# A decoder block whose cross-attention general path moves to the program's end, with the second projection inside the last batch's period

## The chip, the core and the metric

The kernel runs on one core of one Trainium2 chip. The metric is the device time of one execution in microseconds. The engines are TensorE (PE in the rows; its weight loads are PEld), VectorE (DVE), ScalarE (ACT), GpSimd (POOL) and SyncE (SP), which here issues every DMA. Each engine runs its own list of instructions in order and waits on semaphores for the others.

## What is computed

A decoder layer for 32 batches of 56 tokens of width 128: self-attention, cross-attention to 1500 context rows with 16 heads of width 8, and eight experts of hidden width 512; each part is added to its input and normalised. Cut to what matters here:

```python
x = layernorm(x + self_attention(x))
x = layernorm(x + cross_attention(x, ctx))       # logits clipped to +-10000; all 1/1500 if any weight is NaN
# experts
probs = softmax(x @ Wr); the two largest count
for e in range(8):
    gate = probs where e is among the two, else 0
    vals, idx = top_k(gate, 560)                  # a capacity per expert
    y[idx] += vals * (relu(x[idx] @ W1[e]) @ W2[e])
x = layernorm(x + y)
```

## The kernel before

**Numbers.** Tokens lie in pairs of batches, `TT` = 112 tokens; `QT` = 4 pairs are a quad of `QC` = 448 tokens, and there are `NQ` = 4 quads. The matrix products of the experts are made of high and low parts: each product costs three matmuls of 448 columns.

**The loop over batches.** After self-attention, `periods` runs `period(b, ...)` for b = -2 to 32 on every engine. A period has `NC` = 12 slots c. In period b, PE makes the scores of batch b (L1063), ACT takes their exponential (L563), PE sums the outputs (L1113, L1117) into bank 6, and between them the maxima and the keys and values of the batches ahead are made (L1049, L1088, L1097). The result of batch b-1 is divided by its sums in period b (ACT copies it at L558, PE spreads the sums at L1076, DVE inverts at L775 and scales at L778). In period 31 nothing is left to prepare for later batches; period 32 only divides the last result.

**The flag.** Then DVE derives from all maxima and sums whether the fast path was valid (L785 to L794), PE sums that over the partitions (L1123), DVE writes `flag_int` (L796), and each engine that has something to do in the general path loads it into a register and branches: the general path (up to L1173 on PE) is only run for a flag of one, and is not run for these inputs. It stands between the loop and all that follows. DVE then releases the rest with `S3["attended"]`.

**Second projection and norm.** For each quad n: `project(n)` on PE (L1179, eight passes), ACT copies with the bias (L617), `turned(n)` turns it (L1186), DVE adds the residual and takes mean and variance (`norm`, L673 to L682), POOL takes the power -1/2 (L493), DVE scales (L687), `transposed(n)` (L1193), ACT makes two copies `x2T` and `x_hi` (L621, L622), POOL makes `x_lo` (L496), and `logits(n)` (L1199). POOL then clears `y_sum` and splits the weights of the first experts (`split_weights`, L503 to L507), whose DMAs SP issues behind the flag.

**Experts.** A unit u is one expert and one quad; there are `UNITS` = 32 units of `FC` = 4 steps. Step (u, f) is `up(u, f)` (three matmuls, L1222 to L1224) and `down(u-1, f)` (three, L1232 to L1234). After each `up`, ACT makes the high part (L637) and DVE the low part (`low_part`, L857). PE may be ahead by little:

```python
pe.wait_ge(S4["hidden_low"], u * FC + (f - 3) + PRIME)     # up
pe.wait_ge(S4["hidden_low"], u * FC + (f + 1) + PRIME)     # down, of unit u-1
```

ACT copies the result of each unit to `results` (L643), POOL multiplies it by the gates (L518), DVE adds it to `y_sum` (L956). In units 0 to 15, which are written out, DVE works at the gates between the low parts: softmax and the two largest (L865 to L897), PE transposes them at step `EARLY` = 10 (L1243), and then a search for the threshold of each expert in `ROUNDS` = 32 rounds: DVE counts (L906), PE sums over the partitions (L1246), DVE takes the decision (L916, L917, L914, later L924, L925). `low_parts(r)` gives the low parts, and so the steps of PE, that stand in a round; 46 steps are shared by the 32 rounds. The final gates go to DRAM and come back broadcast (`gate_rows`); only then can POOL gate anything. Units 16 to 31 are a hardware loop of two passes, in which DVE does two additions in each unit. In the end PE turns `y_sum` (L1265), DVE normalises quad by quad, and SP stores (L394).

## Time and profile before

| what | value |
|---|---|
| device time, median of three runs | 1047.92 us (1046.09 to 1053.0) |
| the profiled execution | 1049.38 us, span 1047.6 us |
| PE busy | 964.7 us, 92% of the span |
| DVE busy | 727.3 us, 69% |
| ACT busy | 636.2 us, 61% |
| POOL busy | 354.5 us, 34% |
| chain that ended last | PE 79%, DVE 7%, issue 5%, POOL 4% |

The profile is one execution, its times count from the start of the span. Busy times of matmuls are modelled and overlap, so the distance between two starts tells more of PE's pace than a duration does. "Issue" in the chain is time in which an engine waited for nothing that the profile shows.

### The profile page before, as it was taken

Reading aid. Unit: us, or ns where it says so; the run is one execution under the profiler, and the core shown is the slowest. Engines: PE = TensorE matmul, PEld = TensorE weight load, DVE = VectorE, ACT = ScalarE, POOL = GpSimd, SP = SyncE. Lnnn points to the kernel's source line nnn. Section 1 sums busy time; section 2 is a strip of 40 time slices with the busy share of each in tenths; the row PEclk is TensorE's granted clock in tenths of the full one; section 3 lists DMA queues with packets and bytes.
Section 4 is the critical chain, followed back from the end, with each engine's and each line's share of the span. In section 5 each row is a group of like instructions: output and inputs, shape, how many; then the busy total and the mean of one; then the engine's idle time right before and its main releaser. Section 6 shows DMA issues by size and latency. Waiting matters only on the chain.

```text
span 1047.6 us, 29217 instructions
## 1 busy us (share of the span) xinstructions
PE 964.7 (92%) x10560; PEld 776.5 (74%) x10560; DVE 727.3 (69%) x1428; ACT 636.2 (61%) x1030; POOL 354.5 (34%) x325
## 2 busy tenths in 40 slices
PE   6579999999999999999999999999995678999993
PEld 5445778778778887787787788877874367989993
DVE  2775777777777777777777677777751457777996
ACT  3303777777777777777777777777763123445551
POOL 7315333322333322333223333223300151117842
PEclk9855999999999999999999999999997859999997
DMA  3058655566655666555666556665441010105201
GB/s 97 0 113 177 133 129 112 121 143 144 143 110 110 137 145 140 128 110 118 150 140 143 110 110 139 143 142 128 90 90 43 0 41 8 34 3 199 88 35 35
DMA packets 41572, 109.55 MB, mean 105 GB/s; under 512 B 15218, under 2 KB 23732, under 8 KB 41524
## 3 DMA queue, kind: packets, MB, share of 16 engines
q1 hardware_dynamic: 41524, 108.93, 46.3%
q8 instruction: 28, 0.46, 0.2%
q14 instruction: 20, 0.16, 0.1%
HBM read 31.32 MB, written 0.97 MB: 31 GB/s over the span
## 4 chain that ended last, share of the span: by engine, by line
PE 79%; DVE 7%; issue 5%; POOL 4%; SPq 2%; DMA 2%; ACT 1%; POOLq 0%; DVEq 0%; ACTq 0%
PE psum L1063 17%; PE psum L1049 17%; PE psum L1113 12%; PE psum L1088 8%; PE psum L1097 8%; PE psum L1117 4%; POOL OS_all L518 3%; PE psum L1179 2%; PE psum L1222 2%; PE psum L1223 1%; PE psum L1224 1%; PE psum L1076 1%; DMA arena<-gate_rows 1%; PE psum L1234 1%; PE psum L1233 1%
## 5 line engine op out<-in xcount | busy, mean ns | idle before, releaser
L752 DVE TENSOR_REDUCE arena<-psum 128x1 f32<-128x500 f32 x672 | 445.6, 672 | 198.9 <-PE psum L1049 198.8
L563 ACT ACTIVATE arena<-psum 125x896 f32<-125x896 f32 x384 | 348.0, 916 | 98.9 <-PE psum L1063 90.9
L1049 PE MATMUL psum<-K_hi,Q_bd 128*128 128x500 f32 x672 | 323.1, 492 | 6.1 <-DVE arena L752 3.5
L462 POOL TENSOR_TENSOR arena<-arena,K_hi 128x500 fp32r<-128x500 f32 x96 | 123.8, 1291 | 399.4 <-ACT K_hi L578 397.5
L1063 PEld LDWEIGHTS psum<-Q_st,K_st 97*125 97x125 f32 x1536 | 221.8, 189 | 30.9 <-issue 10.9
L1063 PE MATMUL psum<-Q_st,K_st 97*125 97x224 f32 x1536 | 241.6, 280 | 2.8 <-ACT arena L563 1.3
L1049 PEld LDWEIGHTS psum<-K_hi,Q_bd 128*128 128x128 f32 x672 | 130.9, 196 | 56.8 <-issue 28.4
L1113 PE MATMUL psum<-arena 125*25 125x168 f32 x3072 | 169.4, 310 | 0.2
L637 ACT ACTIVATE K_st<-psum 128x448 fp32r<-128x448 f32 x128 | 69.7, 545 | 87.2 <-PE psum L1224 86.7
L1117 PE MATMUL psum<-arena 125*9 125x56 f32 x3072 | 117.1, 213 | 0.0
L1088 PEld LDWEIGHTS psum<-WvA,arena 97*125 97x125 f32 x768 | 103.5, 195 | 4.2
L1117 PEld LDWEIGHTS psum<-arena 125*9 125x9 f32 x3072 | 94.2, 91 | 15.6
L1088 PE MATMUL psum<-WvA,arena 97*125 97x128 f32 x768 | 103.9, 280 | 0.0
L1097 PE MATMUL psum<-arena,WkA 97*128 97x500 f32 x186 | 96.6, 601 | 0.8 <-ACT arena L576 0.8
L1113 PEld LDWEIGHTS psum<-arena 125*25 125x25 f32 x3072 | 69.1, 103 | 33.7 <-issue 32.2
L857 DVE SCALAR_TENSOR_TENSOR K_st<-psum,K_st 128x448 fp32r<-128x448 f32 x128 | 75.1, 617 | 15.2 <-ACT K_st L637 14.9
L481 POOL TENSOR_TENSOR Q_st<-arena,four_heads 96x896 fp32r<-96x896 f32 x32 | 53.7, 1678 | 78.3 <-PE psum L1063 57.5
L576 ACT COPY arena<-psum 128x500 f32<-128x500 f32 x93 | 53.8, 578 | 41.2 <-PE psum L1049 21.7
L592 ACT COPY arena<-psum 125x384 f32<-125x384 f32 x96 | 46.7, 487 | 39.6 <-PE psum L1088 36.3
L775 DVE RECIPROCAL arena<-psum 128x112 f32<-128x112 f32 x64 | 53.8, 842 | 19.6 <-PE psum L1076 19.6
L578 ACT CAST K_hi<-arena 128x500 fp32r<-128x500 f32 x93 | 56.7, 609 | 3.0
L1222 PE MATMUL psum<-K_hi,K_st 128*128 128x448 f32 x128 | 51.2, 400 | 6.1 <-issue 4.1
(246 smaller groups left out, 1056.5 us busy)
## 6 DMA issues: line engine op xcount, KB each, us to landing
K_st<-K_hi SPq DMA_DIRECT2D x256, 187.5 KB, 4.7
K_st<-arena SPq DMA_DIRECT2D x128, 187.5 KB, 3.4
arena<-in_ctx SPq DMA_DIRECT2D x32, 562.5 KB, 6.8
arena<-gate_rows SPq DMA_DIRECT2D x8, 896.0 KB, 4.3
arena<-in_L_ffn_W SPq DMA_DIRECT2D x16, 256.0 KB, 3.1
Q_st<-max_row SPq DMA_DIRECT2D x224, 0.5 KB, 1.7
arena<-K_st SPq DMA_DIRECT2D x12, 224.0 KB, 4.8
out<-x_all SPq DMA_DIRECT2D x4, 224.0 KB, 2.5
```

Of the source, the lines that this page charges most:

```text
L462: g.tensor_tensor(low.bitcast(F32R), low, K_hi[:, par, n * KB:n * KB + KB].bitcast(F32), ALU.subtract).then_inc(F["keys_low"], 1)
L563: a.activation(P2[c % NP].rearrange("p (n k) -> p n k", n=2), psum[0:CK, 2 + 2 * (c % 2):4 + 2 * (c % 2), 0:HQ // 2], ACT.Exp)\
L637: a.activation(h_hi[k % 2][:, f], bank[f][:, 0:QC], ACT.Relu).then_inc(S4["hidden_high"], 1)
L752: v.reduce_max(mx[:, n // NB, n % NB:n % NB + 1], bank_of(n)[:, 0:KB], AX.X).then_inc(F["piece_max_taken"], 1)
L857: v.scalar_tensor_tensor(h_lo[k % 2][:, f], bank[f][:, 0:QC], 0.0, h_hi[k % 2][:, f].bitcast(F32), ALU.max, ALU.subtract)\
L1049: mm(bank_of(n)[:, 0:KB], Q_bd[:, p].rearrange("p h q -> p (h q)")[:, 128 * (n // NB):128 * (n // NB) + 128], K_hi[:, p, (n % NB) * KB:(n ...
L1063: last = mm(bank[2 + 2 * (c % 2) + g // 2][0:CK, 4 * S * (g % 2):4 * S * (g % 2) + 4 * S], K_st[0:DC + 1, par, g, c * CK:c * CK + CK], Q_s ...
L1088: last = mm(bank[7][0:CK, 128 * k:128 * k + 128], ctxT2[:, (par + ahead) % 2, CK * q:CK * q + CK], WvA[:], start=True, stop=True)
L1097: mm(bank[7][:, 0:KB], WkA[:], ctxT2[:, par, n * KB:n * KB + KB], start=True, stop=True).then_inc(F["keys_made"], 1)
L1113: mm(bank[6][32 * m:32 * m + V3, 0:3 * S], values[:, k, V3 * m:V3 * m + V3], weights_[:, 3 * S * m:3 * S * m + 3 * S], start=(k == 0), sto ...
L1117: last = mm(bank[6][32 * m:32 * m + V1, 3 * S:4 * S], values[:, k, 4 * V3 + V1 * m:4 * V3 + V1 * m + V1], weights_[:, (12 + m) * S:(13 + m ...
L1222: mm(bank[f][:, 0:QC], w1_hi[p[0]][:, w_cols], x_hi[:, cols], start=True, stop=False)
```

## The change

- The flag, the branches and the general path stand behind the experts. The flag is made on DVE in unit 24 and summed on PE in unit 26. The fast path's experts run for every input, and the outputs are stored; then each engine loads the flag and branches over the general path, which now holds its own copy of projection, norm and experts (`passes[1]`). For it the first norm's result is saved to DRAM (`x1_rows`, 896 KB) ahead of the loop, since the second norm now works in place.
- Projection, norm and transposes of quads 0 to 2 and the logits of quads 0 and 1 stand in period 31, with DVE making the copies that ACT made. Batch 31's sums, the logits of quad 2 and all of quad 3 stand among the first eleven steps of the experts. POOL splits the first weights in period 31, and SP loads them as soon as batch 31's queries are spread.
- The gates' transpose stands at step 22; 44 steps are shared by the 32 rounds. A round's decision is one instruction: `expert_rows` has weight 4 and a matmul with `level` subtracts the capacity beforehand in PSUM, so that the total is positive or negative by more than any candidate, and clamping it between two bounds gives the next candidate. The bounds are made behind the count, one instruction in 23 rounds and two in seven.
- Nothing is in a hardware loop behind the batches. 24 results are held instead of 16 (`held`). DVE's additions begin in unit 20 and are spread over twelve units, at most one after each low part. POOL gates units 0 to 29, DVE itself the last two, from PSUM (`gate`). `y_sum` lies where `x2T` lay, so that the residual is in it from the start: POOL's clearing and DVE's four last residual additions are gone, and `statistics` and `scaled` read PSUM. The last norm begins for quad 0 while units 30 and 31 are open.

The core of the diff, in the order SP, POOL, ACT, DVE, PE behind the constants:

```diff
-EARLY, BETWEEN = 10, 46
+LEAD, EARLY, BETWEEN = 11, 22, 44
+KEEP = 24
+GATED = UNITS - 2
+WEIGHT = 4.0
+ADD_FROM = 20
...
+P_AT, T_AT, X_AT, LOGITS_AT = 3, 5, 9, 11
+P_BANK, T_BANK, X_BANK, Y_BANK = (0, 1, 1, 6), (7, 7, 7, 5), (0, 0, 4, 6), (6, 7, 0, 1)
+FLAG_AT = 24
...
+        y_sum = x2T.rearrange("p (q n) -> p q n", q=NQ)
...
+            sp.wait_ge(S1["normed"], NQ + PRIME)
+            sp.dma_start(x1_rows, x1_all[:]).then_inc(x1_saved, 16)
...
+            sp.wait_ge(F["stacked_spread"], B + PRIME)
...
-            for e in range(NE - 2):
...
+                for e in range(NE - 1):
+                    load_weights(e)
...
+            with sp.If(clamped > 0):
+                sp.sem_inc(second, 1)
+                sp.dma_start(x1_all[:], x1_rows).then_inc(x1_back, 16)
...
-            pool.wait_ge(F["flag_ready"], 1 + PRIME)
...
+                for n in range(GATED):
+                    if n in (8, 18):
+                        split_weights(P, NE - 2 if n == 8 else NE - 1)
+                    e = n // NQ
+                    pool.wait_ge(G_[e % 2], (P.past * (NE // 2) + e // 2 + 1) * 16)
+                    pool.wait_ge(S4["result_copied"], n + 1 + P.base4["result_copied"])
+                    g.tensor_tensor(held(n), held(n), gates[e % 2][:, n % NQ], ALU.mult).then_inc(S4["result_gated"], 1)
+                for n in range(NQ):
+                    power(S4, P.base4, n)
+            pool.wait_ge(F["scores_made"], (B - 1) * NC + PRIME)
+            split_weights(passes[0], 0)
+            power(S3, passes[0].base3, 0)
+            power(S3, passes[0].base3, 1)
+            low_inputs(passes[0], 0)
+            low_inputs(passes[0], 1)
+            power(S3, passes[0].base3, 2)
+            low_inputs(passes[0], 2)
+            power(S3, passes[0].base3, 3)
+            low_inputs(passes[0], 3)
+            experts(passes[0])
...
+                        if u * FC + f == LEAD + 2:
+                            act.wait_ge(S4["logits_shifted"], 1 + P.base4["logits_shifted"])
+                            a.activation(pw[:], pr[:], ACT.Exp).then_inc(S4["exp_done"], 1)
...
+                    if isinstance(b, int) and b == B - 1:
+                        P = passes[0]
+                        if c in (1, 2, 6):
+                            projected(P, (1, 2, 6).index(c))
+                        if c == 3:
+                            dve.wait_ge(x1_saved, 16)
+                        if c in (3, 4, 9):
+                            attended(P, (3, 4, 9).index(c))
+                        if c in (5, 8, 10):
+                            n = (5, 8, 10).index(c)
+                            scaled(P.S3, P.base3["rstd_ready"], n, quads3[n], x1_all[:, tiles(n), :])
+                        if c in (7, 8, 11):
+                            normed(P, (7, 8, 11).index(c))
...
+                for n in range(LEAD):
+                    if first and n == T_AT:
+                        attended(P, NQ - 1)
+                    if first and n == X_AT - 1:
+                        scaled(P.S3, P.base3["rstd_ready"], NQ - 1, quads3[NQ - 1], x1_all[:, tiles(NQ - 1), :])
+                    low_part(n // FC, n // FC, n % FC)
...
-                step(v.tensor_scalar(cand[:], thr[:], 2.0 ** -(s - 1), None, ALU.mult))
-                step(v.tensor_scalar(fac[:], tot, float(CAP), bit, ALU.is_ge, ALU.mult))
-                step(v.scalar_tensor_tensor((cand if s < 22 else thr)[:], fac[:], less, cand[:], ALU.subtract, ALU.add))
...
+                    def bounds():
+                        last_of(v.tensor_scalar(low_high[:], offsets[:, s], cand[:], None, ALU.add))
+                    tot = count(ALU.is_ge, cand[:], bounds)
+                    step(v.tensor_scalar((cand if s < 22 else thr)[:], tot, low_high[:, 0:1], low_high[:, 1:2], ALU.max, ALU.min))
...
+                def gate(n):
+                    dve.wait_ge(G_[1], 16 * (NE // 2) * (P.past + 1))
+                    dve.wait_ge(S4["result_made"], n + 1 + P.base4["result_made"])
+                    v.tensor_tensor(held(n), bank[4 + n % 2][:, 0:QC], gates[1][:, n % NQ], ALU.mult).then_inc(S4["result_gated"], 1)
+
+                def due(u):
+                    return (u + 1 - ADD_FROM) * GATED // (UNITS - ADD_FROM) if u >= ADD_FROM - 1 else 0
+                for u in range(UNITS // 2, UNITS):
...
+                    if first and u == FLAG_AT:
...
+                ended(0)
+                gate(GATED)
+                add(GATED)
+                ended(1)
+                scaled(S4, P.base4["rstd_ready"], 0, quads3[0], total(0))
+                gate(GATED + 1)
+                add(GATED + 1)
+                scaled(S4, P.base4["rstd_ready"], 1, quads3[1], total(1))
+                ended(2)
+                ended(3)
+                for n in range(2, NQ):
+                    scaled(S4, P.base4["rstd_ready"], n, quads3[n], total(n))
...
-                for a2 in range(2):
-                    n = u * 2 + (a2 - UNITS)
-                    dve.wait_ge(S4["result_gated"], n + 1 + PRIME)
-                    dve.wait_ge(S4["result_added"], n - (NQ - 1) + PRIME)
-                    q = (2 * k + a2) % NQ
-                    v.tensor_tensor(y_sum[:, q], y_sum[:, q], results[:, 2 * k + a2], ALU.add).then_inc(S4["result_added"], 1)
...
+                    if isinstance(b, int) and b == B - 1:
+                        P = passes[0]
+                        if c in (1, 2, 5):
+                            n = (1, 2, 5).index(c)
+                            pe.wait_ge(F["outputs_scaled"], (n + 1) * (B // NQ) + PRIME)
+                            if n == 0:
+                                pe.wait_ge(F["piece_max_taken"], B * PIECES + PRIME)
+                            elif n == 1:
+                                pe.wait_ge(F["max_row_ready"], B + PRIME)
+                            else:
+                                pe.wait_ge(P.S3["projected_copied"], n + P.base3["projected_copied"])
+                            project(P, n)
+                        if c in (3, 4, 8):
+                            if c == 3:
+                                pe.wait_ge(F["sums_inverted"], 2 * b + PRIME)
+                            turned(P, (3, 4, 8).index(c))
+                        if c in (7, 8):
+                            crossed(P, (7, 8).index(c))
+                        if c == 9:
+                            pe.wait_ge(P.S3["residual_added"], NQ - 1 + P.base3["residual_added"])
+                        if c in (9, 11):
+                            logits(P, (9, 11).index(c))
...
+            crossed(passes[0], 2)
...
+                def added(n):
+                    pe.wait_ge(S4["result_added"], UNITS - NQ + n + 1 + P.base4["result_added"])
+                    for t in range(QT):
+                        last = t_.transpose(bank[Y_BANK[n]][0:TT, D * t:D * t + D], y_sum[:, n, TT * t:TT * t + TT], ident[:])
+                    last.then_inc(S4["outputs_made"], 1)
...
+                        if first and u * FC + f == 1:
+                            sums(B)
+                        if first and u * FC + f == 2:
+                            logits(P, 2)
+                        if first and u * FC + f == P_AT:
+                            pe.wait_ge(F["outputs_scaled"], B + PRIME)
+                            project(P, NQ - 1)
+                        if first and u * FC + f == T_AT:
+                            turned(P, NQ - 1)
+                        if first and u * FC + f == X_AT:
+                            crossed(P, NQ - 1)
+                        if first and u * FC + f == LOGITS_AT:
+                            logits(P, NQ - 1)
...
+                added(0)
+                for f in range(FC):
+                    down(UNITS - 1, UNITS - 1, f, 1)
+                    if f == 1:
+                        added(1)
+                for n in range(2, NQ):
+                    added(n)
+            experts(passes[0], True)
```

In the order of PE's instructions, the place between the second and the sixth slot of period 31. `OS_all` is the cross-attention's result, `WoP` the projection's weights. Before:

```order
L1063 MATMUL psum<-Q_st,K_st 125x224 x4
L1076 MATMUL psum<-arena,sum_rows 128x224
L1063 MATMUL psum<-Q_st,K_st 125x224 x8
L1113 MATMUL psum<-arena 25x168 x4
L1117 MATMUL psum<-arena 9x56 x4
```

With the change:

```order
L1246 MATMUL psum<-Q_st,K_st 125x224 x4
L1204 MATMUL psum<-arena,sum_rows 128x224
L1246 MATMUL psum<-Q_st,K_st 125x224 x4
L1208 MATMUL psum<-OS_all,WoP 128x448 x4
L1246 MATMUL psum<-Q_st,K_st 125x224 x4
L1208 MATMUL psum<-OS_all,WoP 128x448 x4
L1311 MATMUL psum<-arena 25x168 x4
L1315 MATMUL psum<-arena 9x56 x4
L1311 MATMUL psum<-arena 25x168 x4
L1315 MATMUL psum<-arena 9x56 x4
L1246 MATMUL psum<-Q_st,K_st 125x224 x4
L1216 MATMUL psum<-ident,arena 112x128 x4
```

The projections of quads 0 and 1 stand ahead of the first outputs (L1311, L1315), and the transpose of quad 0 (L1216) behind the fourth slot's scores.

PE right behind the loop. Before:

```order
L1113 MATMUL psum<-arena 25x168 x4
L1117 MATMUL psum<-arena 9x56 x4
L1076 MATMUL psum<-arena,sum_rows 128x224
L1123 MATMUL psum<-arena,ones 128x1
L1125 TENSOR_LOAD flag_int
L1125 ISA x2
L1126 COMPARE_AND_BRANCH
```

With the change:

```order
L1315 MATMUL psum<-arena 9x56 x4
L1224 MATMUL psum<-ident,x_all 128x112 x4
L1334 MATMUL psum<-K_hi,K_st 128x448
L1335 MATMUL psum<-Q_bd,K_st 128x448
L1336 MATMUL psum<-K_hi,K_st 128x448
L1204 MATMUL psum<-arena,sum_rows 128x224
L1334 MATMUL psum<-K_hi,K_st 128x448
L1335 MATMUL psum<-Q_bd,K_st 128x448
L1336 MATMUL psum<-K_hi,K_st 128x448
L1230 MATMUL psum<-Wr_sb,arena 112x8 x4
```

The flag's matmul, load and branch are gone from here; the experts' first `up` (L1334 to L1336) stands right behind quad 2's transpose, and the last sums (L1204) behind it.

DVE at the end of the 23 rounds of the search. Before:

```order
L924 TENSOR_SCALAR arena<-psum,bits 128x1
L925 SCALAR_TENSOR_TENSOR arena<-arena,bits 128x1
L906 TENSOR_SCALAR arena<-arena 128x112
L857 SCALAR_TENSOR_TENSOR K_st<-psum,K_st 128x448
L924 TENSOR_SCALAR arena<-psum,bits 128x1
```

With the change:

```order
L963 TENSOR_SCALAR arena<-psum,low_high 128x1
L934 TENSOR_SCALAR arena<-arena 128x112
L961 TENSOR_SCALAR low_high<-offsets,arena 128x2
L873 SCALAR_TENSOR_TENSOR K_st<-psum,K_st 128x448
L963 TENSOR_SCALAR thr<-psum,low_high 128x1
```

Between a total and the next count (L906, now L934) stands one instruction instead of two, and the bounds (L961) stand behind the count.

## Rows read from the trace of the kernel before

**Rows 1.** Stretches: busy (count) of PE, PEld, DVE, ACT, POOL; clock, DMA, GB/s.

```profile
780.00:797.40 17.40, 14.43 (x291) 11.46 (x290) 1.97 (x4) 11.88 (x16) 0.00 (x0) 1.00 0.01 2
...
808.60:853.00 44.40, 27.39 (x97) 18.03 (x97) 18.95 (x67) 6.71 (x13) 14.73 (x14) 0.69 0.04 12
853.00:860.00 7.00, 7.00 (x21) 6.30 (x22) 4.90 (x10) 2.72 (x5) 4.42 (x4) 0.56 0.47 136
...
869.00:873.00 4.00, 4.00 (x16) 3.63 (x15) 1.82 (x9) 1.21 (x3) 0.00 (x0) 0.57 0.00 0
873.00:941.00 68.00, 64.45 (x338) 58.06 (x338) 51.98 (x181) 31.51 (x58) 13.64 (x12) 1.00 0.06 17
941.00:1026.00 85.00, 84.46 (x418) 78.36 (x419) 73.42 (x103) 45.38 (x86) 54.54 (x42) 1.00 0.28 100
```

**Rows 2.** Chain that ended last, loop's end to experts: start us, us, what.

```profile
797.38 0.35 ACT arena L558
...
803.85 0.55 DVEq L798
...
804.83 3.22 issue
...
818.36 3.01 PE psum L1179 x8
...
852.98 0.71 PE psum L1222
```

**Rows 3.** Timeline, projection and norm: start us, us, engine, line, operation.

```profile
821.20 0.60 PE L1186 MATMUL psum<-ident,arena 128*112 128x128 f32 x4
...
821.84 0.69 DVE L673 TENSOR_TENSOR arena<-psum,x_all 112x512 f32<-112x512 f32 x1 [1.23 <-PE psum L1186]
...
842.18 1.53 PE L1199 MATMUL psum<-Wr_sb,arena 128*112 128x8 f32 x8
```

**Rows 4.** Timeline, PE, two steps apart by one, late in the experts.

```profile
1002.32 0.37 PE L1222 MATMUL psum<-K_hi,K_st 128*128 128x448 f32 x1
...
1003.53 0.37 PE L1222 MATMUL psum<-K_hi,K_st 128*128 128x448 f32 x1
```

**Rows 5.** Groups by line, 941 to 1029 us: busy us, mean ns, idle before.

```profile
L857 DVE SCALAR_TENSOR_TENSOR K_st<-psum,K_st 128x448 fp32r<-128x448 f32 x74 | 42.8, 615 | 10.8 <-ACT K_st L637 10.6
...
L956 DVE TENSOR_TENSOR Qt_all<-Qt_all,OS_all 128x448 f32<-128x448 f32 x31 | 34.8, 1158 | 2.6 <-POOL OS_all L518 2.6
```

**Rows 6.** Timeline, additions with POOL busy beside them, and alone.

```profile
961.45 5.27 POOL L518 TENSOR_TENSOR OS_all<-OS_all,arena 128x448 f32<-128x448 f32 x4
...
964.21 2.99 DVE L956 TENSOR_TENSOR Qt_all<-Qt_all,OS_all 128x448 f32<-128x448 f32 x2
...
1028.84 0.63 DVE L956 TENSOR_TENSOR Qt_all<-Qt_all,OS_all 128x448 f32<-128x448 f32 x1 [1.46 <-POOL OS_all L518]
```

**Rows 7.** Timeline, one round of the search: decision, count, and PE's wait ahead.

```profile
868.32 0.32 PE L1243 MATMUL psum<-ident,arena 112*128 112x112 f32 x1 [2.49 <-DVE arena L897]
...
928.59 0.22 DVE L924 TENSOR_SCALAR arena<-psum,bits 128x1 f32<-128x1 f32 x1 [0.93 <-PE psum L1246]
...
929.10 0.33 DVE L906 TENSOR_SCALAR_CACHE_REDUCE arena<-arena 128x112 f32<-128x112 f32 x1
```

**Rows 8.** Timeline, final gates stored, and POOL's first gating behind them.

```profile
940.98 0.33 SPq L385 DMA_DIRECT2D gate_rows<-arena  x1
...
946.80 9.32 POOL L518 TENSOR_TENSOR OS_all<-OS_all,arena 128x448 f32<-128x448 f32 x8 [10.77 <-DMA arena<-gate_rows]
```

**Rows 9.** Timeline, SP's first DMA behind the branch, and the end.

```profile
804.87 0.37 SPq L375 DMA_DIRECT2D arena<-in_L_ffn_W  x1
...
1026.59 0.37 PE L1232 MATMUL psum<-K_st 128*128 128x448 f32 x1
...
1031.64 0.68 DVE L673 TENSOR_TENSOR arena<-psum,x_all 112x512 f32<-112x512 f32 x1
...
1042.17 2.36 DVE L687 TENSOR_SCALAR x_all<-arena 112x128 f32<-112x128 f32 x8
```

741 lines of the change are left out of this document (399 added, 342 removed).

## The prediction

> **What bounds the kernel now.** I read the stretches first. In the experts' second half PE is busy 84.46 of 85.00 us [rows 1]; its matmuls stand 1.213 us apart from step to step, 1002.32 to 1003.53 [rows 4], which is six matmuls at 0.202. 85.00 / 1.213 is 70 steps, and about that many are there: that stretch runs at PE's pace. The loop is close to PE's pace too, but its last period is not full: 14.43 of 17.40 us. The hole lies between: from 797.40 to 808.60 PE works 1.24 us, from 808.60 to 853.00 only 27.39 of 44.40, at a granted clock of 0.69 (between the levels of 1.2 and 2.4 GHz) [rows 1]. The chain of waits says why: batch 31's copy at 797.38, then DVE's small instructions for the flag until 803.85, then a branch with 3.22 us of "issue", then projections and norms in turn, then the first expert matmul at 852.98 [rows 2].
>
> **The gap goes.** From 797.38 to 852.98 are 55.6 us [rows 2]. All of it leaves its place; what comes back is counted next.
>
> **Period 31 gets longer.** PE now has in it three projections, 3 x 3.0 (the one with eight passes, 3.01 [rows 2]); three transposes into PSUM, 3 x 0.5 (0.60 at a middling clock [rows 3]); two transposes back, 2 x 0.5 by the same row; and the logits of two quads, 2 x 1.0 (1.53 at the low clock [rows 3]; I take two thirds). That is 13.5. PE's idle time there is 17.40 - 14.43 = 3.0 [rows 1], but in pieces that belong to waits on ACT, and two new waits for DVE come (the second transpose needs the bank that DVE reads, the transposes back wait for POOL's power and DVE's scaling), about 2 us in all. I count +14 and let the idle time absorb no more than these waits; bounds 10.5 (all 3.0 filled, no wait) and 18. DVE has little else to do there, 1.97 us of 17.40, and ACT 11.88 [rows 1], so the norm's chain, some 4 us a quad (0.69 for the addition alone [rows 3]), can lie beside scores. The loop ends at 797.4 + 14 = 811.4.
>
> **Behind the loop.** Between the first eleven steps stand quad 2's transpose back 0.5, batch 31's sums 0.5, logits 1.0, quad 3's projection 3.0, transposes 0.5 and 0.5, logits with the level's matmul 1.2, by the same rows: 7.2. Step 3 waits for DVE's inversion and scaling of batch 31, step 9 for the norm of quad 3; DVE has nine low parts of 0.615 [rows 5] in the same time. I add 1.3 for both: +8.5.
>
> **The experts.** Ideal are 4 x 0.6 for unit 0, 124 x 1.213 and 4 x 0.6 for the last `down`, 155.3 us. Before, they took 852.98 to 1026.59 + 2.4 = 1029.0, or 176.0: 20.7 more [rows 2, 9]. Of that I can name: the low clock behind the gap, 21 matmuls in 7.00 us instead of 4.2 [rows 1], 2.8; the wait of 2.49 for the gates ahead of the transpose [rows 7] and 4.00 us for 16 matmuls behind it at a clock of 0.57 [rows 1], 0.8 too many; the counts' own matmuls, 33 x 0.14 = 4.6, where 0.14 is my reading of such a small pair; the rest, some 10, is in the rounds and at the loop's ends. What I take after:
> - the low clock is gone, as PE has no gap ahead of the experts; counts 4.6 stay (the subtracting matmul is one more small one a round, inside this figure's error).
> - At step 22 DVE has had twelve more low parts' time for the gates' work, but begins it later (logits of quad 3 at step 11). The 2.49 becomes about 1.6, and I leave the clock behind it at full.
> - The rounds: a decision after a total is now one instruction of 0.22 and not two; between the decision at 928.59 and the count at 929.10 lay 0.51 [rows 7], so some 0.25 a round leaves DVE's serial chain and 0.2 comes back for `bounds`, off the total's path. PE waits for a total's round only where low parts run out; I give the rounds 2.5 in all (0 to 6).
> - The additions. Before, 31 in 85 us took 1.158 each on average [rows 5]; alone one takes 0.63, and two beside POOL's four gatings of 5.27 took 2.99, 1.5 each [rows 6]. Now all 30 lie in twelve units, 2.5 a unit. A unit of DVE is 4 x 0.58 (0.615 with its share of the contention [rows 5]) + 2.5 x 1.17 = 5.25, against PE's 4 x 1.213 = 4.85. POOL begins to gate at about 917 (below) and has 30 x 1.32 [rows 6] + two splits of 5 = 50 us, so it is busy until some 966, which covers units 20 to 27: 8 x 0.4 = 3.2. The flag's chain in unit 24 is ten small DVE instructions, 2.5 us. The low parts have about 3 us of lead. 3.2 + 2.5 - 3 = 2.7, and I take 4, as single waits don't average out; bounds 0 and, with every addition at 1.5 (2.32 + 3.75 = 6.07, 1.2 over, 8 units), 10.
>
> The sum of waste is 4.6 + 1.6 + 2.5 + 4 = 12.7, taken as 13, for 20.7. The gates in time: steps 0 to 73 lie by 811.4 + 8.5 + 73 x 1.213 and waste of 7 at about 915; the gates' way out and back took 940.98 to 946.80 [rows 8], so POOL starts at 917. DVE's first addition is at unit 20, 925; POOL is then six gatings on, and gains, so additions don't wait for it.
>
> **The end.** Before, from the end of step 127 (1026.59) to the span's end are 21.0. DVE's work there went from 1031.64 to 1042.17 + 2.36 = 1044.53, 12.9, and 3.1 came behind it [rows 9]. Four residual additions of 0.69 [rows 3] go, two gatings and two additions of 0.63 to 0.69 come: 12.9 - 2.8 + 2.6 = 12.7, with 0.5 for waits on PE 13.2. DVE may be 2.5 behind PE at step 127 (a unit's last low part, an addition, and 1.2 for PE's transposes of quad 0). 2.5 + 13.2 + 3.1 = 18.8.
>
> **The branch at the end.** It costs between 1.1 (SP's first DMA at 804.87, 1.0 behind DVE's 803.85 [rows 2, 9]) and 4.2 (803.85 to the end of the 3.22 "issue" at 804.83 [rows 2]). Most engines reach it long before the last output lands, and the stores' 3.1 can cover some of it; I take 2. The Trainium skill ("Runtime: NRT & Kernel Launch", section "Instruction fetch mechanics") has instructions prefetched in sequence only, so a branch over a long piece has to fetch; by it the larger value holds on every run, and the sum would be 2 higher. The 3.22 of "issue" agrees, but PE alone shows it here.
>
> **Free edits.** Saving `x1_rows` (896 KB) rides on queues at 0.01 to 0.06 of their time in the late loop [rows 1]; early there is room of some microseconds before the next loads, by the order of SP; if it collides, +1. The weights' loads start under period 31 where the DMA share is 0.01 [rows 1].
>
> **The sum.** 811.4 + 8.5 + (155.3 - 2.4) + 13 = 985.8; + 18.8 + 2 = 1006.6, against the span of 1047.6: -41.0. The profiled execution took 1.8 more than its span, the median 1047.92 is 1.5 below the profiled one. I lay the difference on the median: 1047.9 - 41.0 = **1007**.
>
> **Rivals.**
> - *A, the forecast:* 1000 to 1016. Chance 0.62.
> - *B, DVE overloaded by POOL.* Each addition waits out a whole gating: 0.63 + 1.12 (most of one of 1.32) = 1.75. A unit is 2.32 + 2.5 x 1.75 = 6.7, 1.85 over; from unit 20 on over twelve units (the late gatings slip too) 22, with 2.5 for the flag and 3 of lead 21.6 instead of 4: 1024. At 1.5 each it is about 1017. For it: 2.99 for two additions beside 5.27 of POOL [rows 6]; against: the mean of 1.158 [rows 5], of times when POOL was busy 54.54 of 85 [rows 1]. The Trainium skill ("SBUF — State Buffer", "Who interferes with whom") has a port shared by DVE's second input and POOL, locked for a whole instruction; by it the 1.75 would be met by nearly each addition while POOL is busy, and the forecast 1024. The 2.99 lies between, nearer to 1.75. Chance 0.17.
> - *C, cheaper than summed:* the period absorbs 3, no overload (-4), rounds free (-2.5), the branch hidden (-1): 995 to 999. For it: each term is a full count of PE's work. Chance 0.13.
> - *D, the norm isn't hidden:* each quad in period 31 is a serial round, 3 x (3 + 1 + 0.6 + 4 + 0.6 + 1.3) = 32 instead of 14: 1025. Against: the order puts other slots' scores between. Chance 0.03.
> - *E, slower:* experts written out in full starve PE of instructions, each refill like the 3.22 of "issue" [rows 2]. It decides from 41 us lost over 32 units on, 1.3 a unit, or 2.6 for each of the sixteen that were a loop; one refill of 3.22 in each of those sixteen is 51.5, which gives 1007 + 51.5 = 1058. Against: units 0 to 15 were written out before and 64.45 of 68.00 us were busy with the rounds in them [rows 1]. Chance 0.03.
> - Something else, 0.02.
>
> **Range and chances.** C's better end and B's worse bound the range: 997 to 1022 leaves out half of C and, of B with D and E, some 0.13. A, B, C and D all are faster by over 1%, which is about what a measurement of this kernel can tell from no change: 0.95 faster, 0.02 the same, 0.03 slower.
>
> **What would show it.** PE's first `up` (L1334) at about 812, with next to no idle time between 797 and 812, and a granted clock of 1.00 from 780 to the end of the experts. A wait of 1.6 ahead of the gates' transpose. The first gating (L547) near 917. The additions (L990) at a mean of 1.17 in units 20 to 27 and below 0.9 behind; if they stand at 1.5 or more with PE waiting for L873, B holds. The last `down` (L1346) at about 989, DVE's last instruction at 1001.5, the end at 1006.6, with a queue's load and branch of at most 4 us behind the last output. I am wrong if PE waits more than 4 us in period 31, or if steps of units 20 to 31 stand over 1.35 apart.

## The result, and the profile after

| what | before | after |
|---|---|---|
| device time, median of four | 1047.22 us (1046.09 to 1053.0) | 1013.56 us (1011.31 to 1015.97) |
| ratio, with its 95% interval | | 0.9663 (0.9638 to 0.9687) |
| the profiled execution, its span | 1049.38, 1047.6 us | 1015.97, 1014.2 us |
| PE busy | 964.7 us, 92% | 959.0 us, 95% |
| DVE, ACT, POOL busy | 727.3, 636.2, 354.5 us | 721.2, 631.3, 349.3 us |

The forecast was 1007, with a range of 997 to 1022. The change takes 34 us off and not 41. The profile after is that of the slowest of its four executions, so a stage that looks long in it is held against a second profile of the same program (`e12_repeat`, span 1010.3) below.

Stretches of the kernel after, columns as in [rows 1]:

```profile
797.40:804.00 6.60, 4.63 (x92) 3.78 (x84) 4.50 (x10) 2.65 (x3) 1.43 (x2) 1.00 0.01 4
804.00:812.00 8.00, 8.00 (x85) 7.01 (x80) 3.82 (x17) 3.67 (x4) 2.16 (x2) 0.53 0.01 2
...
846.00:855.00 9.00, 5.44 (x18) 4.58 (x18) 5.87 (x24) 1.63 (x3) 2.90 (x3) 0.66 0.20 58
855.00:905.00 50.00, 50.00 (x267) 45.84 (x266) 37.73 (x143) 23.95 (x44) 9.11 (x8) 0.99 0.08 22
905.00:925.00 20.00, 17.17 (x89) 15.48 (x89) 16.19 (x43) 8.71 (x16) 4.54 (x4) 1.00 0.06 13
```

The gap of [rows 2] is gone: PE is busy 8.00 of 8.00 us where it had stood still. Three smaller holes are left: 2.0 us at 797 to 804, 3.6 at 846 to 855, 2.8 at 905 to 925, and two of them have a low clock (0.53, 0.66) beside or behind them. TensorE's clock has two levels, 1.2 and 2.4 GHz; a value between 0.50 and 1.00 is a stretch that has both. The timeline of PE gives the waits, with the starts of some steps (L1334 is the first matmul of an `up`):

```profile
802.89 0.60 PE L1224 MATMUL psum<-ident,x_all 112*128 112x112 f32 x4 [1.79 <-DVE x_all L731]
...
814.71 0.45 PE L1334 MATMUL psum<-K_hi,K_st 128*128 128x448 f32 x1
...
832.86 0.45 PE L1334 MATMUL psum<-K_hi,K_st 128*128 128x448 f32 x1
...
845.20 0.37 PE L1334 MATMUL psum<-K_hi,K_st 128*128 128x448 f32 x1
...
850.14 0.45 PE L1378 MATMUL psum<-ident,arena 112*128 112x112 f32 x1 [3.56 <-DVE arena L919]
850.27 0.72 PE L1334 MATMUL psum<-K_hi,K_st 128*128 128x448 f32 x1
...
918.04 0.37 PE L1334 MATMUL psum<-K_hi,K_st 128*128 128x448 f32 x1
...
922.25 0.47 PE L1334 MATMUL psum<-K_hi,K_st 128*128 128x448 f32 x1 [2.83 <-DVE K_st L873]
...
995.16 0.37 PE L1334 MATMUL psum<-K_hi,K_st 128*128 128x448 f32 x1
```

The L1334 rows are the starts of steps 0, 11, 21, 22, 69, 70 and 127. With the starts in between, the program can be laid beside the forecast stage by stage, in both profiles of it:

| stage, by starts of PE | forecast | after | repeat |
|---|---|---|---|
| start of period 31's scores | 782.9 | 780.45 | 780.61 |
| first `up` (step 0) | 811.9 | 814.71 | 810.06 |
| to step 11 | 18.9 | 18.15 | 18.11 |
| to step 21 | 12.1 | 12.34 | 12.34 |
| to step 24 (gates' transpose) | 5.2 | 10.4 | 9.5 |
| to step 66 (the rounds) | 57.7 | 58.5 | 58.4 |
| to step 72 (final gates) | 7.6 | 10.7 | 12.2 |
| to step 127 | 71.0 | 70.4 | 70.1 |
| to the end of the span | 22.1 | 19.0 | 19.6 |

Two stages are 3 to 5 us longer than forecast, one is 3 shorter, and the first `up` moves between the two executions by 4.7. The repeat's final gates take 1.5 more than those of the profile after because the clock fell there behind the same wait: it was 0.79 in the 8 us from 916.6, and 1.00 in those from 922.2 in the profile after. DVE and POOL show what is behind the 2.83. Timeline of DVE, then of POOL, at the final gates:

```profile
917.11 0.91 DVE L980 TENSOR_SCALAR arena<-arena 128x112 f32<-128x112 f32 x1
918.05 1.02 DVE L981 TENSOR_TENSOR arena<-arena 128x112 f32<-128x112 f32 x1
919.11 1.31 DVE L982 TENSOR_TENSOR arena<-arena 128x112 f32<-128x112 f32 x1
920.45 1.22 DVE L983 TENSOR_TENSOR arena<-arena 128x112 f32<-128x112 f32 x1
```

```profile
917.90 1.04 POOL L532 TENSOR_TENSOR K_st<-arena,ones 128x512 fp32r<-128x512 f32 x1
919.02 1.26 POOL L534 TENSOR_TENSOR K_st<-arena,K_st 128x512 fp32r<-128x512 f32 x1
920.24 1.29 POOL L535 TENSOR_TENSOR K_st<-arena,K_st 128x512 fp32r<-128x512 f32 x1
...
927.73 3.37 POOL L547 TENSOR_TENSOR OS_all<-OS_all,arena 128x448 f32<-128x448 f32 x3 [6.20 <-DMA arena<-gate_rows]
```

And the same instructions in the kernel before (L941 and L942 there), where POOL's split had ended at 936:

```profile
940.06 0.28 DVE L941 TENSOR_TENSOR arena<-arena 128x112 f32<-128x112 f32 x1
940.37 0.27 DVE L942 TENSOR_TENSOR arena<-arena 128x112 f32<-128x112 f32 x1
```

Each of DVE's instructions ends within 0.15 us of one of POOL's. The change moved the split of expert 5 and the final gates against each other until they met. The low parts of step 66 and on stand behind these four in DVE's list, and PE waits for them.

### The profile page after: what moved, and what is told of

It reads as the page before. It is cut to its first block, busy times and chain, and to the rows that moved or that the text cites. A ratio compares the mean times of both kernels' runs of the same rounds, so it can differ in the third digit from the quotient of the medians.

```text
span 1014.2 us, 28901 instructions
## 1 busy us (share of the span) xinstructions
PE 959.0 (95%) x10562; PEld 771.5 (76%) x10562; DVE 721.2 (71%) x1440; ACT 631.3 (62%) x1019; POOL 349.3 (34%) x322
## 4 chain that ended last, share of the span: by engine, by line
PE 87%; DVE 8%; SPq 2%; issue 1%; DMA 1%; ACT 1%; POOL 0%; DVEq 0%; ACTq 0%
PE psum L1246 17%; PE psum L1195 17%; PE psum L1311 12%; PE psum L1286 8%; PE psum L1295 8%; PE psum L1315 4%; PE psum L1334 3%; PE psum L1335 2%; PE psum L1336 2%; PE psum L1346 2%; PE psum L1347 2%; PE psum L1348 2%; PE psum L1208 1%; PE psum L1204 1%; SPq L365 1%
## 5 line engine op out<-in xcount | busy, mean ns | idle before, releaser
L1311 PE MATMUL psum<-arena 125*25 125x168 f32 x3072 | 170.8, 312 | 0.1
L1315 PE MATMUL psum<-arena 125*9 125x56 f32 x3072 | 117.7, 214 | 0.0
L1315 PEld LDWEIGHTS psum<-arena 125*9 125x9 f32 x3072 | 94.8, 92 | 16.0
L1311 PEld LDWEIGHTS psum<-arena 125*25 125x25 f32 x3072 | 69.5, 104 | 34.4 <-issue 33.6
L501 POOL TENSOR_TENSOR Q_bd<-Qt_all,head_rows 128x896 fp32r<-128x896 f32 x32 | 54.6, 1709 | 1.9 <-DVE Qt_all L804 1.8
```

The costliest lines, as they stand in the source:

```text
L1311: mm(bank[6][32 * m:32 * m + V3, 0:3 * S], values[:, k, V3 * m:V3 * m + V3], weights_[:, 3 * S * m:3 * S * m + 3 * S], start=(k == 0), sto ...
L1315: last = mm(bank[6][32 * m:32 * m + V1, 3 * S:4 * S], values[:, k, 4 * V3 + V1 * m:4 * V3 + V1 * m + V1], weights_[:, (12 + m) * S:(13 + m ...
```

## The experiments

Each run is timed against the kernel before on the same chip; a ratio is to that. Single executions of one program lie 1.5 to 10 us apart here, so stages are compared in the profiles and the whole by ratios. The baseline is the change's own 0.9663 (repeat: 0.9641).

**Quad 1's transpose back at slot 9.**

```diff
-                        if c in (7, 8):
-                            crossed(P, (7, 8).index(c))
+                        if c in (7, 9):
+                            crossed(P, (7, 9).index(c))
```

with `normed` on DVE moved alike.

> One edit: in period 31 the transpose back of quad 1 on PE, and the copies that DVE makes of it, move from slot 8 to slot 9. Theory: in the changed kernel PE waited 1.79 us there for DVE's scaling of quad 1 (itself stretched from 1.11 to 1.94 us beside a POOL subtraction), and behind that wait the granted clock was 0.53 from 804 to 812; both go, so the first up (L1334) stands at about 809 to 810 instead of 814.7, and the time falls by 4 to 6 us, from 1013.6 to about 1008.5. Rival one: the low clock has nothing to do with this wait: only the wait goes, first up at about 813, 1012. Rival two: the wait moves to slot 9 or 11 and the clock falls there: no change, 1013.6.

1010.24 us, 0.9622 (0.9588 to 0.9655). The wait of 1.79 is gone, and one of 1.10 stands ahead of quad 2's transpose instead, with the clock at 0.82 in 804 to 812. From period 31's first scores to the first `up` it takes 29.7 us (780.18 to 809.87), as in the repeat (29.4). This is rival two: the wait and the low clock moved, and the ratio does not tell the run from the baseline.

**The exponential earlier.**

```diff
-                        if u * FC + f == LEAD + 2:
+                        if u * FC + f == LEAD:
```

> One edit: ACT takes the gates' exponential at step 11 (ahead of that step's high part) and not at step 13. In the changed kernel DVE stood idle 2.31 us for it at 833 to 835.7. Theory: the gates are ready about 2 us earlier, PE's wait ahead of the gates' transpose at step 22 falls from 3.7 to some 1.7 us; whether the clock behind it (0.53 for about two steps, 2.9 us lost) still falls decides between -2 (1011.6) and -5 (1008.7). Rival: the gates' chain is bound by DVE's own instructions, the idle time only moves to a low part that waits for ACT: 1013.

1013.65 us, 0.9668 (0.9636 to 0.9699). The theory failed and the rival holds. DVE's idle time of 2.31 went, but PE waits 3.57 us at step 22 as before: DVE now waits for low parts. The low part of step 21 can't come before PE has made step 21, and behind it in DVE's list stand five more instructions of the gates. That tail, not the sum of DVE's work, is what PE waits for.

**The gates' transpose at step 28.**

```diff
-LEAD, EARLY, BETWEEN = 11, 22, 44
+LEAD, EARLY, BETWEEN = 11, 28, 36
```

with four more of the gates' instructions followed by a low part.

> One edit: the gates' transpose stands at step 28 and not 22, six more low parts stand between the gates' instructions, and 36 steps instead of 44 are shared by the 32 rounds. Theory: PE does not reach the transpose before the gates are there; the wait of 3.7 us and the low clock behind it (2.9) go: -6, to 1007.5, if the rounds stay bound by PE. Rival: with 1.125 steps to a round the rounds are bound by their own chain (total, decision, count, about 1.4 us and more of low parts), PE waits in each, and what was gained is given back: 1013 or more.

1001.79 us, 0.9569 (0.9525 to 0.9612). From step 21 to 72 it takes 72.3 us against 79.6 and 80.1. PE's wait at the transpose:

```profile
847.65 0.31 PE L1378 MATMUL psum<-ident,arena 112*128 112x112 f32 x1 [1.52 <-DVE arena L919]
```

In the 4 us behind the end of this wait the clock stays at 1.00, where it is 0.50 and 0.57 in the two profiles of the kernel after. The final gates come two steps earlier here, their four instructions at 0.28 us each, and POOL's split behind them. So this one edit takes away both holes, and its 8 us (7.3 and 7.8 by the stages, 7.5 to 10 by the ratios) are not the price of the first alone. The rounds, with 1.125 steps each, gave little back.

**No general path at the end.**

```diff
-            clamped = pe.value_load(flag_int[0:1, 0:1], min_val=0, max_val=1)
-            with pe.If(clamped > 0):
```

and all under it, on five engines.

> The changed kernel without the general path at its end: the flag is still made, but no engine loads it or branches, and the general path's code is left out. Theory of the forecast: the load and the branch cost 2 us at the end, so 1011.6. Rival one, that they are hidden behind the last stores: below 1 us, 1013. Rival two, that each engine pays the full issue time of 4.2 at the end: 1009.4.

1009.39 us, 0.963 (0.9596 to 0.9663). DVE's last instruction to the end of the span takes 3.0 us (1002.97 to 1006.0), where the kernel after takes 3.9 and the repeat 4.4. So load and branch cost 0.8 to 1.4 us at the end; the ratios say 1 to 3.5, but with the noise above. That is neither the 4.2 of rival two nor much less than 1 us. The stores may cover the rest, as the forecast held; no run separates that.

**The kernel before without its general path.** The same lines are removed, on the four engines that have them, behind the loop.

```diff
             pe.wait_ge(F["flag_ready"], 1 + PRIME)
-            clamped = pe.value_load(flag_int[0:1, 0:1], min_val=0, max_val=1)
-            with pe.If(clamped > 0):
```

> The kernel before without the general path between the loop and the experts: the flag is still made and waited for, but no engine loads it or branches, and the general path's code is left out. Theory: from 803.85 (DVE's load) to 808.61 (first projection) 4.75 us were load, branch and issue, of which some 0.3 stay as the semaphore's way: -4.4, 1043. Rival: the branch also leaves the clock low behind it (0.69 and 0.56 in the stretches to 860), so that more than 6 us go: 1040. Rival two: the stretch behind is bound by SP's weights (issued at 804.87, used at 848): only what the projections gain, again -4.4, or nothing if POOL's chain bounds: 1047.

1041.98 us, 0.9952 (0.9927 to 0.9978). The chain of waits between the flag's matmul and the first projection:

```profile
799.79 0.60 PE psum L1049 x2
800.71 7.92 PE psum L1056 x16
```

0.92 us, where before the flag's matmul started at 803.04 and the projection at 808.61 [rows 2]: 4.65 less. The profiled execution, the fastest of the eight, has another 3.0 us less between period 31's first scores and the first expert matmul (62.4 in all against 70.1), so rival one, more than 6 us, is not excluded by it; the median, 5 us with an interval from 2 to 8, lies between the theory and the rival. So of the 55.6 us of the gap the branch was worth about 5; it is the work behind it, and the order it stood in, that made the rest.

**One more instruction in each decision.**

```diff
                     step(v.tensor_scalar((cand if s < 22 else thr)[:], tot, low_high[:, 0:1], low_high[:, 1:2], ALU.max, ALU.min))
+                    step(v.tensor_scalar(fac[:], tot, low_high[:, 0:1], low_high[:, 1:2], ALU.max, ALU.min))
```

> The changed kernel with one more DVE instruction (the same clamping, into an unused column) and its wait in each of 30 rounds, 0.28 us and 0.03 of issue each: nearly the decision of the kernel before again. Theory: the rounds of the changed kernel stand 1.95 us apart with PE all but full, so of 30 x 0.31 = 9.3 us about a third to a half shows: +3 to +5, 1017. Rival one, PE alone bounds the rounds: no change, 1013.6 (then the one-instruction decision bought nothing). Rival two, the chain of total, decision and count bounds each round: +9, 1023.

1016.0 us, 0.9713 (0.9688 to 0.9739), about 5 above the baseline's ratio. From step 24 to 66 it takes 64.9 us against 58.5. DVE in one round, and PE's wait there:

```profile
868.53 0.27 DVE L964 TENSOR_SCALAR arena<-psum,low_high 128x1 f32<-128x1 f32 x1
868.84 0.28 DVE L965 TENSOR_SCALAR arena<-psum,low_high 128x1 f32<-128x1 f32 x1
869.15 0.33 DVE L934 TENSOR_SCALAR_CACHE_REDUCE arena<-arena 128x112 f32<-128x112 f32 x1
```

```profile
869.54 0.38 PE L1383 MATMUL psum<-arena,expert_rows 128*128 128x1 f32 x2 [0.36 <-DVE arena L934]
```

Of 9.3 us added to DVE's chain 6.4 show on PE. The rounds stand at the edge: PE is full in the kernel after (50.00 of 50.00 us), yet each 0.3 us more in the chain costs 0.2. With the instruction added PE is busy 46.48 of 50.00 us in the same stretch: the one-instruction decision is what keeps it full.

**Period 31's additions behind the loop.**

```diff
             periods(pe, period)
+            for c in range(NC):
+                if c in (1, 2, 5):
...
+                if c in (9, 11):
+                    logits(P, (9, 11).index(c))
             crossed(passes[0], 2)
```

The block goes from period 31 on PE, and DVE's to the start of period 32.

> The changed kernel with the three projections, turns, norms and logits that stood in period 31 behind the loop instead, in the same order on PE and on DVE, the rest unchanged. Theory of the forecast (the norm's chain is covered by period 31's scores and outputs): the PE work is the same, but PE now waits for DVE and POOL between its pieces, some 4 us for quads 0 and 1, 2 for quad 1's scaling, 3 for quad 2's norm, and the 3 us of idle time that period 31 had come back: +9 to +13, with a low clock behind the waits up to +16: 1023 to 1030. Rival (the chain was not covered in period 31 either): within 3 us of 1013.6.

1020.97 us, 0.9753 (0.9722 to 0.9784), 9 above the baseline's ratio. The chain of waits behind the loop:

```profile
806.96 0.87 DVE arena L720 x4
807.97 0.29 DVE arena L724 x3
808.36 1.12 DVE x_all L731 x4
809.52 0.62 PE psum L1224 x4
...
811.32 1.85 DVE x_all L731 x4
813.22 1.02 PE psum L1224 x4
```

The norm's chain is bare here, and scores and outputs cover it in the kernel after. The first `up` stands at 820.5 and not at 810 to 815. That is the theory's sign and the lower end of its size. Part of the 9 is the clock, which was 0.50 from 812.9 to 820.5.

**POOL's split behind the final gates.**

```diff
                 for e in range(1, NE - 2):
+                    if e == 5:
+                        pool.wait_ge(S4["gates_final"], 1 + P.base4["gates_final"])
                     split_weights(P, e)
```

> The changed kernel with one wait more: POOL splits the weights of expert 5 only when the final gates are made. In the changed kernel this split (917 to 921.6) lay beside DVE's last four instructions of the gates, which took 0.91, 1.02, 1.31 and 1.22 us; in the kernel before, with POOL at rest, the same four took 0.28 each. Theory: the two engines hold each other up; the four take 1.15 us again instead of 4.5, PE's wait of 2.83 at step 68 goes and POOL gates 3 us earlier: -3, 1010.6. Rival: they are slow for another reason (the low parts' traffic or the state of the buffers): the durations stay, and the time stays or grows as expert 5's weights come later: 1013.6 to 1016.

1006.81 us, 0.9629 (0.9601 to 0.9656). DVE, then POOL (its lines are two further down, L982 to L985 are the four):

```profile
911.12 0.28 DVE L983 TENSOR_TENSOR arena<-arena 128x112 f32<-128x112 f32 x1
911.44 0.28 DVE L984 TENSOR_TENSOR arena<-arena 128x112 f32<-128x112 f32 x1
911.75 0.28 DVE L985 TENSOR_TENSOR arena<-arena 128x112 f32<-128x112 f32 x1
```

```profile
912.10 1.04 POOL L531 TENSOR_TENSOR K_st<-arena,ones 128x512 fp32r<-128x512 f32 x1 [19.00 <-DVE arena L985]
...
917.94 8.93 POOL L549 TENSOR_TENSOR OS_all<-OS_all,arena 128x448 f32<-128x448 f32 x8 [1.18 <-DMA arena<-gate_rows]
```

A wait added on POOL makes the program faster: the four are at 0.28 again, PE's wait of 2.83 is gone, and steps 66 to 72 take 7.6 us as forecast and not 10.7 to 12.2. That is 3.1 us with the clock at full and 4.6 with the fall; the whole gains 3.5 by the first ratio of the kernel after and 1.3 by the repeat's. The first gating is at 917.9. The collision is shown as the cause of this hole.

**Both splits behind the gates.**

```diff
                 for e in range(1, NE - 2):
+                    if e == 2:
+                        pool.wait_ge(S4["gates_ready"], 1 + P.base4["gates_ready"])
+                    if e == 5:
+                        pool.wait_ge(S4["gates_final"], 1 + P.base4["gates_final"])
```

> As the run in which POOL's split for expert 5 waits for the final gates (1006.8), and the split for expert 2 waits for the first gates as well. In the changed kernel and in that run it lay beside DVE's last instructions of the choice of two experts (0.78, 0.74 and 1.23 us where the same kinds take 0.28 alone). Theory: these 1.9 us go, so PE's wait ahead of the gates' transpose falls from 3.6 to some 1.7, and the time by 2, or by up to 4 if the clock then stays at full: 1003 to 1005. Rival: the chain is held by the low parts before it, the wait stays: 1006.8.

1002.75 us, 0.9567 (0.9525 to 0.9608). The two instructions of DVE had taken 0.73 and 1.23 in the kernel after, beside the split of expert 2:

```profile
847.13 0.73 DVE L909 TENSOR_TENSOR arena<-arena 112x128 f32<-112x128 f32 x1
847.90 1.23 DVE L914 TENSOR_TENSOR arena<-arena 112x128 f32<-112x128 f32 x1
```

```profile
846.46 1.26 POOL L534 TENSOR_TENSOR K_st<-arena,K_st 128x512 fp32r<-128x512 f32 x1
847.67 1.30 POOL L535 TENSOR_TENSOR K_st<-arena,K_st 128x512 fp32r<-128x512 f32 x1
```

In this run, PE's wait ahead of the transpose, then the same two:

```profile
842.98 0.32 PE L1382 MATMUL psum<-ident,arena 112*128 112x112 f32 x1 [2.17 <-DVE arena L923]
```

```profile
841.35 0.28 DVE L913 TENSOR_TENSOR arena<-arena 112x128 f32<-112x128 f32 x1
841.67 0.29 DVE L918 TENSOR_TENSOR arena<-arena 112x128 f32<-112x128 f32 x1
```

Of the wait of 3.57 these were 1.4; the 2.17 left is the tail itself. The clock still fell behind it (0.68 in the 4 us from 842.98). Steps 21 to 72: 74.2 us, against 76.6 with the one split.

**All together:** the edits of slot 9, exponential, transpose at 28 and both splits.

> All edits of the single runs together: quad 1's transpose back at slot 9, the exponential at step 11, the gates' transpose at step 28 with 36 steps shared by the rounds, both splits behind the gates. Theory: the gains of the transpose's place (-8 by the traces, of which -3 is the final gates' collision that the split's wait takes away too), of the splits (-3.5, shared) and of slot 9 (-1.8) give 1013.6 - 5 - 3.5 - 1.8 - 1 = 1002, or 1000 with the exponential's 2 us now useful because PE still waited 1.5 there. Rival: with fewer steps to a round the rounds fall back on their own chain and the sum is no better than the single run's 1001.8.

1000.21 us, 0.9547 (0.9504 to 0.959), the fastest program here, 11.2 us below the repeat in the same comparison. Steps 21 to 72 take 72.2 us, as with the transpose at 28 alone (72.3): that move had taken both collisions away already. The rest is within the noise.

**No flag.**

```diff
-                    if first and u == FLAG_AT:
-                        dve.wait_ge(F["outputs_scaled"], B + PRIME)
...
-                    if first and u == FLAG_AT + 2:
-                        dve.wait_ge(F["bad_summed"], 1 + PRIME)
...
-                            mm(bank[7][:, 0:1], ones[:], bad[:, 0:1], start=True, stop=True).then_inc(F["bad_summed"], 1)
```

on top of the run without the general path.

> The changed kernel without general path, branch and flag: the flag's eleven DVE instructions and its matmul are left out too. Against the run without the general path alone (1009.4), this prices the flag's chain in unit 24 beside the additions and the gatings. Forecast's term: 2.5 of DVE time, of which the lead of the low parts hides some: -2 to -3, 1007. Rival: it is stretched by POOL's gatings (0.79, 0.64 and 1.05 us in it where others take 0.15) and costs PE all of it, -3.5. Rival two: the additions after it catch up in the slack: 0, 1009.4.

1004.96 us, 0.9603 (0.9551 to 0.9656). Stretches of this run, units 20 to 31:

```profile
925.00:945.00 20.00, 20.00 (x101) 18.55 (x100) 16.33 (x24) 10.96 (x21) 16.89 (x15) 1.00 0.26 93
945.00:985.50 40.50, 40.50 (x202) 37.58 (x201) 36.45 (x56) 22.70 (x42) 29.89 (x22) 1.00 0.24 92
```

PE does not wait at all. Steps 72 to 127 take 66.7 us, which is 55 x 1.213 exactly, against 70.3 in the run without the general path and 70.4 and 70.1 in the kernel after. The additions cost nothing, the flag's chain costs 3.5 us here; in the other runs that have the flag the stretch takes 68.8 to 70.7, which makes it 2 to 4. The ratio (0.9603 against 0.963) has the sign, but its interval covers no change. The first rival's cause shows in the trace of the kernel after, in the flag's chain and in PE's wait for it:

```profile
962.08 0.79 DVE L1014 TENSOR_TENSOR arena<-arena 128x1 f32<-128x1 f32 x1
...
963.47 0.64 DVE L1018 TENSOR_TENSOR arena<-arena,sum_row 128x1 f32<-128x1 f32 x1
964.14 1.05 DVE L1019 TENSOR_TENSOR arena<-arena 128x1 f32<-128x1 f32 x1
```

The ten instructions take 4.7 us and not 2.5, with POOL's split of expert 6 and its gatings beside them, and PE waits 1.02 us for the last one. It looks like a third collision of the same kind, but that is argued from the other two places; no run moved POOL away here.

**The change once more.**

> The changed kernel itself once more. In its first profile the granted clock was 0.53 from 804 to 812, behind a wait of 1.79 us in period 31, and 0.66 behind the wait of 3.7 at step 22. Three other kernels whose code is the same in period 31 had the same wait and a clock of 1.00 behind it. Theory: the low clock in period 31 comes in some executions and not in others, and is worth 4.5 us (814.7 against 807 to 808 for the first up): the median is again 1013 to 1014 with executions from 1009 to 1016. Rival: it belongs to this program's code, and every profile of it shows the clock low there.

1011.39 us, 0.9641 (0.9597 to 0.9685). Stretches of its profile:

```profile
797.40:804.00 6.60, 4.65 (x57) 3.47 (x59) 4.58 (x9) 2.34 (x3) 1.52 (x2) 0.80 0.00 0
804.00:812.00 8.00, 8.00 (x126) 7.00 (x116) 4.37 (x18) 4.01 (x7) 2.24 (x3) 0.95 0.01 2
```

The median came 2 us below what was expected. The wait is 1.77 us as it was, and the first `up` stands 4.7 us earlier. The clock fell here too, but sooner and for less long: 0.80 in the first stretch and 0.95 in the second. Counted from the end of the wait, the clock of the next 8 us was 0.60 in the profile after, 0.79 in the repeat, and in seven other runs with the same code in period 31 it was 1.00 three times and 0.80 to 0.86 four times. From there to the first `up` it took 7.4 us in the three at full clock, 8.6 to 8.8 in the five between, and 11.8 in the profile after. So the wait is there in each execution, the low clock in six of nine, and it costs 1.3 us, or 4.5 in the one long fall.

## Why the prediction held, and where it was off

**The gap.** 55.6 us left its place, as forecast. The branch alone was about 5 of them; period 31's cover was worth 9 (the serial run, with some of it the clock).

**Period 31, +14.** From its scores to its end the period took 14.5 us before (782.9 to 797.4). In the run without the general path, whose clock stayed at full, it took 27.8 (778.7 to 806.4), in the repeat 29.1, in the profile after 33.6: +13.3, +14.6 and +19.1, the last outside the bound of 18. The term was right at full clock. What it left out is that the clock can fall inside it: in the profile after 4.5 us behind the wait of 1.79 and some 1.7 at the period's start (clock 0.66 from 780 to 785, 1.00 in the repeat). That was read over nine profiles, not produced at will: taking the 1.79 away only moved it. PE's waits in the period sum to 2.5 us, as the 2 of the forecast and under its sign of 4.

The start of the period was luck. The sum took 782.9 from the profile before; the profiles of the changed kernel have 780.5 and 780.6, all its variants lie between 778.6 and 781.7, and the kernel before without its branch, whose loop is unchanged, has 779.7. So 2.3 us that the change did not earn hide as much of the misses.

**Behind the loop, +8.5.** Measured 18.15 against 18.9 for the stretch to step 11: right, 0.7 too much.

**Step 22.** The term of the forecast that failed: a wait of 1.6, and "I leave the clock behind it at full". The wait was 3.56 and the clock fell; 10.4 and 9.5 us for three steps instead of 5.2. Taken from the old wait less an improvement, the figure had no list behind it. The list shows what sets it: the low part of step 21, then five instructions (1.6 us when POOL is at rest), stretched to 3.0 beside POOL's split. Of the 2.0 us by which the wait was longer than forecast 1.4 are this stretch and 0.6 the tail; the other 2 to 3 us of the stage are mostly the clock. Both halves were readable before: the order of the changed kernel has the split of expert 2 at step 20.

**The rounds, +7.1 with the counts.** 58.5 against 57.7: right. The extra decision says that without the clamping they would have cost some 6 more.

**The final gates.** Not in the sum. The collision with the split of expert 5 cost 3.1 us, and 4.6 in the repeat, where the clock fell behind the wait; the first gating came at 927.7 and not 917. It was rival B's mechanism at a place where the forecast did not look.

**Additions and flag, 4.** The size was right (3.7 and 3.4 over 55 steps) by luck, since both its terms were wrong: 3.2 for the additions was 0, and 2.5 for the flag was 3.5 (of a chain that took 4.7 and not 2.5). Groups of the kernel after, 925 to 964 and 964 to 996 (mean ns behind the busy time):

```profile
L990 DVE TENSOR_TENSOR arena<-arena,OS_all 128x448 f32<-128x448 f32 x12 | 12.0, 1001 | 0.0
...
L990 DVE TENSOR_TENSOR arena<-arena,OS_all 128x448 f32<-128x448 f32 x10 | 8.5, 849 | 0.0
...
L990 DVE TENSOR_TENSOR arena<-arena 128x448 f32<-128x448 f32 x8 | 5.3, 660 | 0.0
```

1.00 and not 1.17: a unit is 2.32 + 2.5 x 1.00 = 4.8, just under PE's 4.85. Single additions did take 1.63, near rival B's 1.75, but not each: for the additions B is refuted.

**The end.** 15.2 us from step 127 to DVE's last instruction, where 16.9 were forecast, since DVE is hardly behind PE there (0.7 and not 2.5); the branch costs 0.8 to 1.4 and not 2. Together 3 us less.

So the forecast was 7.6 below the span of the profile after, by +3 at the loop's end, +5 and +3 at the two collisions and -3 at the end; and it was 3.7 below that of the repeat, by -2, +4, +5 and -2.5 at the same places. Rival C had the tail's sign, D is refuted (period 31 covers the chain), E never showed: PE is busy 40.50 of 40.50 us in code written out. The median lies in the forecast's own range with errors of both signs in it. The holes at the final gates and a part of that at step 22 have the cause that the forecast had priced for the additions only.

## What to carry to other kernels

When an edit shifts work on one engine against another, list what each of DVE and POOL does in the new neighbourhood: a chain of short DVE instructions that others wait for must not lie beside POOL's elementwise work, and one wait on POOL, which has time, can be worth more than the edit. A wait at a hand-over is set by what stands in the list behind the last thing that depends on the waiting engine, so count that tail, or move the hand-over until it is hidden. And price additions at the rate of their own neighbourhood, not at the mean of a stage.

## What the runs showed of the hardware

- A short DVE instruction with two SBUF operands took up to as long as POOL's instruction beside it: 0.28 us alone, 1.02 to 1.31 beside POOL's 1.04 to 1.29, and 0.28 again when POOL waits. Even those of one column (L1014, L1018, L1019) took 0.64 to 1.05, where one without POOL beside it (L967) took 0.16. A `tensor_scalar` from SBUF (L980) took 0.91, one of 112x128 by four (L731) 1.94 and not 1.11. The low parts, with one operand in PSUM, stayed at 0.60 to 0.63, all 128 of them. The Trainium skill ("SBUF — State Buffer", section "Who interferes with whom") says this: the port pair is locked for a whole instruction, with two SBUF inputs or in a two-port mode. The runs agree; what the forecast missed is that the rule weighs most on short instructions, since the wait does not shrink with them, while an addition of 0.63 paid only 0.4 more in the mean of units 20 to 27.
- Behind one and the same wait of PE of 1.8 us in the same code the granted clock of the next 8 us was 1.00 in three executions, 0.79 to 0.86 in five and 0.60 in one, which cost nothing, 1.3 and 4.5 us. Behind a wait of 1.52 the clock stayed at 1.00 in both profiles that have it; behind 2.17 it fell in the one; behind 2.8 it fell in six of eight; behind 3.56 or 3.57 it fell in each of nine.
- Load and branch over a long piece cost 4.65 us where PE waits for the flag, and 0.8 to 1.4 at the end, beside the last stores.
